# A shifted-window attention and expert block on one core: the channel norm once per token, with the normalised x, v and the gates passed through memory

## The reference

```python
x = x + _L0_conv_ref(_ln_c(x), qkv_w, lepe_w, bias_table)
t = _to_tokens(x)
t = t + _L0_ffn_ref(_ln_t(t), router_w, router_b, expert_w, expert_b)
```

## Time and profile before

| | us |
|---|---|
| median of three runs | 3803.37 |
| lowest, highest | 3798.1, 3808.32 |
| profiled execution, its own time | 3802.88 |
| its span, first to last instruction | 3801.0 |
| busy: PE, DVE, POOL, ACT | 3274.6, 3207.6, 2920.3, 2223.4 |

### The profile page before, as it was taken

The page is one execution under the profiler, slowest core; times in us unless marked ns, Lnnn a source line. Parts: engine busy times, 40 slices in busy tenths (PEclk is TensorE's granted clock), DMA queues, the critical chain, the costliest instruction groups (busy, mean ns, idle before and its releaser), DMA issues.

```text
span 3801.0 us, 207759 instructions
## 1 busy us (share of the span) xinstructions
PE 3274.6 (86%) x83621; PEld 1990.9 (52%) x83621; DVE 3207.6 (84%) x7044; ACT 2223.4 (58%) x4516; POOL 2920.3 (77%) x5385
## 2 busy tenths in 40 slices
PE   3889898888888888888888988888888898889985
PEld 1655555555555555555555555555555555555541
DVE  2789988888888888988888888888888888999983
ACT  2666655665656656565566665666565665666641
POOL 3988878787878777878787877787787878888860
PEclk8999999999999999999999999999999999999985
DMA  1232323232323222323222232322232323233221
GB/s 32 59 81 73 82 70 82 70 82 68 83 70 80 71 76 76 78 75 78 72 74 78 74 78 72 80 75 78 69 81 69 82 71 82 73 84 79 76 65 39
DMA packets 307856, 279.35 MB, mean 73 GB/s; under 512 B 122368, under 2 KB 288304, under 8 KB 306864
## 3 DMA queue, kind: packets, MB, share of 16 engines
q1 hardware_dynamic: 140976, 152.09, 15.2%
q0 software_dynamic: 165888, 113.57, 12.0%
HBM read 95.33 MB, written 56.62 MB: 40 GB/s over the span
## 4 chain that ended last, share of the span: by engine, by line
PE 25%; SPq 22%; DVE 20%; issue 16%; DMA 10%; ACT 5%; DVEq 1%; POOL 1%; POOLq 0%; ACTq 0%
SPq L401 14%; SPq L433 7%; PE bank L629 6%; DMA z2t<-z 6%; DVE lepe L929 4%; DMA z<-fin 4%; PE bank L584 3%; PE bank L634 3%; PE bank L561 3%; DVE fin L989 3%; PE bank L656 3%; DVE gx L917 2%; PE bank L543 2%; DVE prob L949 2%; ACT row_inv L701 2%
## 5 line engine op out<-in xcount | busy, mean ns | idle before, releaser
L490 POOL DMA_DIRECT2D vx<-vt x3072 | 1555.3, 515 | 623.8 <-issue 487.2
L629 PEld LDWEIGHTS bank<-probT,vx 128*32 128x32 f32 x36864 | 827.9, 191 | 254.1 <-issue 250.4
L629 PE MATMUL bank<-probT,vx 128*32 128x16 f32 x36864 | 888.7, 235 | 25.2 <-issue 23.6
L479 POOL DMA_DIRECT2D kx<-k_sb x1536 | 737.8, 488 | 119.3 <-ACT k_sb L748 100.3
L561 PEld LDWEIGHTS bank<-kx,qx 32*32 32x32 f32 x36864 | 571.6, 109 | 330.6 <-issue 326.9
L561 PE MATMUL bank<-kx,qx 32*32 32x64 f32 x36864 | 673.8, 221 | 54.3 <-issue 46.1
L929 DVE SCALAR_TENSOR_TENSOR lepe<-vpad,lepe_sb,lepe 128x384 f32<-128x384 f32 x960 | 675.8, 704 | 0.0
L917 DVE TENSOR_TENSOR gx<-bank,yn_pair 128x384 f32<-128x384 f32 x768 | 424.2, 552 | 280.6 <-PE bank L532 277.6
L543 PE MATMUL bank<-gx,expert_sb 128*64 128x384 f32 x1536 | 343.1, 526 | 173.2 <-DVE gx L917 171.3
L725 ACT ACTIVATE prob<-prob 128x512 f32<-128x512 f32 x576 | 359.8, 625 | 199.3 <-DVE prob L949 189.9
L509 POOL TENSOR_TENSOR lepe_p<-lepe_p,tap_sb 128x384 f32<-128x384 f32 x384 | 424.7, 1106 | 27.5 <-issue 6.1
(11 more groups left out here) (101 smaller groups left out, 4803.6 us busy)
## 6 DMA issues: line engine op xcount, KB each, us to landing
vx<-vt POOLq DMA_DIRECT2D x3072, 12.0 KB, 1.9
kx<-k_sb POOLq DMA_DIRECT2D x1536, 24.0 KB
yn_pair<-yn POOLq DMA_DIRECT2D x384, 96.0 KB
z<-fin SPq DMA_DIRECT2D x1344, 24.0 KB
xs<-in_x SPq DMA_DIRECT2D x96, 192.0 KB
xt<-in_x SPq DMA_DIRECT2D x192, 96.0 KB
z0t<-z SPq DMA_DIRECT2D x192, 96.0 KB
out_y<-y_out SPq DMA_DIRECT2D x192, 96.0 KB, 2.2
```

Of the source, the lines that this page charges most:

```text
L479: pool.dma_start(kx[to + m:to + C:4, r % 2, m, :], k_sb[at + m:at + C:4, r % 2, :])\
L490: pool.dma_start(vx[to:to + TOK, r % 2, g * 8 + x:g * 8 + 8:2, odd, :], vt[at:at + TOK, r % 2, x::2, :, :].rearrange("p h n k -> p h (n k)"))\
L629: last = MM(bank_o[32 * c:32 * c + 32, at * TOK:(at + 1) * TOK], vx[:, kr % 2, :, at % 2, at // 2 * 4 + c], probT[:, kr % 2, at, c * TOK:( ...
```

## The change

**The channel norm** is now done once per tile on unrolled tokens. SP loads x into a new buffer xa (two DMAs), centre, variance and the multiply run on xa once a tile in place of once a strip, SP stores the result to memory as xn (two DMAs, store_xn) and loads the strips, rolled and unrolled, from xn into xs (five DMAs, load_strips, seven slots later).

**v** goes from vt through memory: two DMAs store it into v_rows (store_v), in pieces of 192 B, and eight DMAs, in place of sixteen, load vx from there in pieces of 1536 B. vx has another order of its axes.

**The gates** are no longer split into bf16 parts. PE transposes them in fp32 (L572's place), ACT copies them, SP stores them (one DMA of 24 KB, store_gates) and loads each row into 64 partitions with four DMAs of 393 KB each (spread_gates) into gate_wide. The eight selection matmuls are gone. gx is made by four DVE operations of 768 columns on inputs that are both in SBUF, and the experts' matmuls follow by pairs. The bias is one fp32 matmul.

**load_tile** moves from SP's queue to POOL's, behind spread_k, store_v, spread_v and pair_yn and before pool_taps in a slot's list. The two additions for y are in two slots; y has four buffers. The logits are transposed into bank_g. The lags grow: the strips' steps from value on by nine slots, store_z from 15 to 24, load_tile from 24 to 34, the first use of the loaded tile from 27 to 37, tile_out from 39 to 56. DVE does gate steps 0 to 11 in the first of two slots and 12 to 16 in the second.

In the diff "..." stands where lines are left out; POOL's load_tile issues the same seven loads as SP's did.

```diff
 LAG = dict(
-    centre=0, variance=1, value=2, query_key=3,
-    spread_k=4, turn_v=5, place_bias=6, spread_v=8, score=7, shift=8,
-    turn_p=10, product=11, divide=14,
-    tap_products=6, pool_taps=7, taps=10, add_taps=15,
-    store_z=15, load_tile=24, tile_sum=27, tile_variance=28, router=29, logits=30, gates=31,
-    pair_yn=31, gap_exp=33, turn_gates=34, experts=35, tile_out=39)
+    centre=0, variance=1, store_xn=2, load_strips=9, value=11, query_key=12,
+    spread_k=13, turn_v=14, store_v=15, place_bias=15, spread_v=17, score=16, shift=17,
+    turn_p=19, product=20, divide=23,
+    tap_products=15, pool_taps=16, taps=19, add_taps=24,
+    store_z=24, load_tile=34, y_first=37, y_second=38, tile_sum=39, tile_variance=40, router=41, logits=42,
+    take_logits=43, gates=45, gap_exp=46, turn_gates=47, pair_yn=47, store_gates=48, spread_gates=50,
+    expert_bias=52, products=53, experts=54, tile_out=56)
...
+PRODUCT_AT = {(0, 1): 0, (1, 0): 1, (1, 1): 2, (2, 0): 3}
+EXPERT_AT = {(0, 0): 0, (1, 0): 1, (1, 1): 2, (2, 0): 3}
...
+        xn = nc.dram_tensor("xn", [B, C, H, W], FP32, kind="Internal").ap()
+        v_rows = nc.dram_tensor("v_rows", [2, 2, 128, 8, WIN // 2 * 4], FP32, kind="Internal").ap()
+        gate_rows = nc.dram_tensor("gate_rows", [2, GE, SPX], FP32, kind="Internal").ap()
...
-        vx = sb("vx", [128, 2, 32, 2, WIN // 2 * 4])
+        vx = sb("vx", [128, 2, 2, 32, WIN // 2 * 4])
...
-        y = sb("y", [128, 2, SPX])
+        y = sb("y", [128, 4, SPX])
...
+        gate_wide = sb("gate_wide", [128, PAIRS, 2, SPX])
...
-        gx = sb("gx", [128, 4, SPX])
+        gx = sb("gx", [128, 2, 2, SPX])
...
+            def load_x(r, im):
+                for half in range(2):
+                    at = (r % IMT * (2 * SP) + half * SP) * W
+                    sp.dma_start(xa[half * C:(half + 1) * C, r % 2, :],
+                                 x_flat[bass.ds(im, 1)][:, :, at:at + SPX].rearrange("b c n -> c (b n)"))\
+                        .then_inc(x_loaded[r % 2], 16)
...
+                if ti := s.tile("store_xn"):
+                    k, r = ti
+                    wait_alone(sp, xn_made, k + 1)
...
+                        sp.dma_start(xn_flat[im][:, :, at:at + SPX].rearrange("b c n -> c (b n)"),
+                                     xa[half * C:(half + 1) * C, r % 2, :]).then_inc(xn_stored[r % 2], 16)
+                if ti := s.tile("load_strips"):
+
+                    k, r = ti
+                    if r % IMT == 0:
+                        wait_alone(sp, xn_stored[r % 2], (k // 2 + 1) * 32)
+                    if r % IMT < IMT - 1:
+                        wait_alone(sp, xn_stored[(r + 1) % 2], ((k + 1) // 2 + 1) * 32)
+                    if s.later(r, 2):
                         wait_alone(sp, k_made, (k - 1) * 2)
-                    load_pair(r, s.image(r, IMT))
+                    im, ring, t = bass.ds(s.image(r, IMT), 1), r % 2, r % IMT
...
+                        sp.dma_start(xs[rows, 2 * ring:2 * ring + 2, :].rearrange("p a n -> p (a n)")[:, at * W:(at + n) * W],
+                                     xn_flat[im][:, src_c, row * W:(row + n) * W]
+                                     .rearrange("b c n -> c (b n)")).then_inc(xs_loaded[ring], 16)
...
+                if ti := s.tile("store_gates"):
+                    k, r = ti
+                    wait_alone(sp, gateT_saved, k + 1)
+                    if s.later(r, 2):
+
+                        wait_alone(sp, gate_spread[r % 2], k // 2 * (GATE_DMAS * 16))
+                    sp.dma_start(gate_rows[r % 2], gateT[:, r % 2, :]).then_inc(gate_stored[r % 2], 16)
+                if ti := s.tile("spread_gates"):
+                    k, r = ti
+                    wait_alone(sp, gate_stored[r % 2], (k // 2 + 1) * 16)
+                    if s.later(r, 1):
+                        wait_alone(sp, gx_made, k * PAIRS)
+                    by_expert = gate_rows[r % 2].rearrange("(f p e) n -> e f p n", f=2, e=2)
+                    for odd in range(2):
+                        for half in range(2):
+                            sp.dma_start(gate_wide[odd * C:(odd + 1) * C, :, half, :],
+                                         by_expert[odd, half].unsqueeze(0).broadcast_to([C, PAIRS, SPX]))\
+                                .then_inc(gate_spread[r % 2], 16)
...
+                if st := s.strip("store_v"):
+                    k, r = st
+                    wait_alone(pool, vt_made, k + 1)
+                    if s.later(r, 2):
+                        wait_alone(pool, v_spread[r % 2], k // 2 * (V_DMAS * 16))
+
+                    for x in range(2):
+                        pool.dma_start(v_rows[r % 2, x, :, x::2, :],
+                                       vt[:, r % 2, x::2, :, :].rearrange("p h n k -> p h (n k)"))\
+                            .then_inc(v_stored[r % 2], 16)
...
-                    wait_alone(pool, vt_made, k + 1)
+                    wait_alone(pool, v_stored[r % 2], (k // 2 + 1) * 32)
...
                     for g in range(4):
                         for x in range(2):
-                            for odd in range(2):
-                                to, at = g * CH + x * TOK, g * CH + odd * TOK
-                                pool.dma_start(vx[to:to + TOK, r % 2, g * 8 + x:g * 8 + 8:2, odd, :],
-                                               vt[at:at + TOK, r % 2, x::2, :, :].rearrange("p h n k -> p h (n k)"))\
-                                    .then_inc(v_spread[r % 2], 16)
+                            rows = v_rows[r % 2, x].rearrange("(g o k) q n -> g k o (q n)", g=4, o=2)[g]
+                            to = g * CH + x * TOK
+                            pool.dma_start(vx[to:to + TOK, r % 2, :, g * 8:(g + 1) * 8, :].rearrange("p o q n -> p o (q n)"),
+                                           rows).then_inc(v_spread[r % 2], 16)
...
+                if ti := s.tile("load_tile"):
+                    k, r = ti
...
+                    for p in range(2):
+                        wait_alone(pool, z_stored[p], counts[p] * (Z_DMAS * 16))
+                    if s.later(r, 2):
+
+                        wait_alone(pool, y_made, k - 1)
...
+                        pool.dma_start(dst[rows, r % 2, at * W:(at + n) * W],
+                                     src[im][:, :, row * W:(row + n) * W]
+                                     .rearrange("b c n -> c (b n)")).then_inc(tile_loaded[r % 2], 16)
...
-                        pe.wait_ge(gx_made, k * E + e)
-                    MM(bank_g[:, 0:SPX], expert_sel[:, e, :], gateT[:, r % 2, :], start=True, stop=True)\
-                        .then_inc(gate_spread, 1)
...
-                    pe.wait_ge(gx_made, k * E + (e + 1))
-                    if e % 2:
-                        for half in range(2):
-                            last = MM(bank_f[half * C:(half + 1) * C, 0:SPX], expert_sb[:, e // 2, :],
-                                      gx[:, (e - 1 + half) % 4, :], start=False, stop=(e == E - 1),
-                                      skip_group_check=True)
-                        last.then_inc(expert_made, 1)
-                    if e + 1 < E:
-                        spread_gate(k, r, e + 1)
+                    pe.wait_ge(gx_made, k * PAIRS + (p + 1))
+                    for half in range(2):
+                        last = MM(bank_f[half * C:(half + 1) * C, 0:SPX], expert_sb[:, p, :], gx[:, p % 2, half, :],
+                                  start=False, stop=(p == PAIRS - 1), skip_group_check=True)
+                    last.then_inc(expert_made, 1)
...
                     for blk in range(TBLK):
-                        last = MM(bank_p[0][0:3 * GE, blk * 128:(blk + 1) * 128],
-                                  gate_part[:, blk, :, :].rearrange("p a b -> p (a b)"), ident_bf[:, :],
-                                  start=True, stop=True)
+                        last = nc.tensor.transpose(bank_g[0:GE, blk * 128:(blk + 1) * 128],
+                                                   gate_tmp[:, 4, blk * GE:(blk + 1) * GE], const("ident"))
...
-                if st := s.strip("variance"):
-                    k, r = st
+                if ti := s.tile("variance"):
+                    k, r = ti
                     pe.wait_ge(sq_made, k + 1)
...
                     MM(bank_p[1][:, 0:SPX], const("mean"), sq[:, r % 2, :], start=True, stop=True).then_inc(var_made, 1)
...
+                    pe.wait_ge(xs_loaded[r // 2 % 2], (k // 4 + 1) * (XS_DMAS * 16))
...
-                if st := s.strip("centre"):
-                    k, r = st
...
-                    MM(bank_p[0][:, 0:SPX], const("centre"), xs[:, r % 4, :], start=True, stop=True).then_inc(xc_made, 1)
+                if ti := s.tile("centre"):
+                    k, r = ti
...
+                    MM(bank_p[0][:, 0:SPX], const("centre"), xa[:, r % 2, :], start=True, stop=True).then_inc(xc_made, 1)
```

(28 more changed lines are left out.)

267 lines of the change are left out of this document (117 added, 150 removed).

## The result

The changed kernel takes 4024.14 us in the median of 4 runs (4020.29 to 4031.06), beside 3800.73 us in the median of 4 runs of the kernel before: a ratio of 1.058 (95% interval 1.0555 to 1.0604), 5.8% slower, where 5% faster was forecast. The profiled execution took 4020.29 us, its span 4018.6.

The account below looks back on a forecast made before the run. Half of the tile was taken as paced by memory, half by DVE and PE. New loop: 95.5 tiles x 35.2 us + 248 us fill and drain = 3610, plus 1.9 outside the span: 3612 us, 5% faster; range 3320 to 3780.

Parts of the forecast that it names:

- The SP part: SP's queue: nine added transfers at 0.6 us, 18.0 us from even fin, so the odd strip's z stores start 2 us late.
- rival (b): Gate broadcast clogs SP's DMA rings, PE waits for xs loads if it takes over 17 us; 4060 us, chance 0.12.
- I cost the v, k, xn paths at nothing: Waits for v, xn and xs transfers to land: two or three slots cover them, so no time added.
- collision term: DVE's gx, now reading two SBUF inputs, collides with POOL's adds: 0.5 us a tile taken, at most 1.9.
- The loop: Odd fin, z stores landed 11.1, POOL 13.7, DVE 10.1: 34.9 us; with a second loop of 34.6, 35.2 a tile.
- then DVE, 10.1: Last part of the loop: DVE from its first tap to the next odd fin, 10.1 us.
- The sign of it: Sign of a right forecast: DVE waits before L929's first tap for POOL's adds, 2 to 3 us a tile.
- floor of 32.4: DVE's least time per tile: 33.1 - 2.2 + 0.5 + 1.0 (other idle time) = 32.4 us.
- Outside the steady part: Fill and drain: 193 us now plus 55 for 17 more light slots, 248 us.
- (a): DVE is the bound and POOL's chain hides: only the floor of 32.4 us remains, 3344 us; chance 0.28.
- (c): v stores cost POOL 4.1 us each, so POOL needs 42 us a tile: 4261 us; chance 0.03.
- (d): Work moves but the loop stays at 37 us through SP's waits and POOL's add: 3793 us, no change; chance 0.04.

## Why the prediction was wrong

**The failed step: the gate copies priced at their issue.** The SP part gave the four copies 0.6 us each and said "their size hardly matters to the issue". That was true (0.62 to 0.65 us) and beside the point: what they do to the other work once issued stood at nothing in the sum, and only rival (b) asked for it. 1.57 MB a tile in one burst keeps all engines full (share 0.81 and more from 1554 to 1569 us in the tile shown). Added alone to the kernel before, this traffic costs 444 us; taking three fourths of it from the kernel after gives 365 us (4024 - 3660). The forecast missed by 412 us.

**The rival that had it.** Rival (b), the broadcast clogs the rings, gave 4060 us at a chance of 0.12; it was 4024. That it came so near is luck, for its mechanism was not the one: it had PE wait for the strip loads, and PE waited 32.3 us for them in all. By its own rule PE should not have waited: the engines were full for some 15 us, under its 17. What it missed is that a full set of DMA engines delays work that has no queue in common with the copies. That PE's instructions are among it is inferred, not shown: no view gives the time at which an instruction arrives. For it speak four things. The stall falls in the middle of a group with nothing named that it waits for. It comes with full engines and not with mere lateness. DVE's five pauses, one a turn of the loop, grow from 10.1 to 39.3 us under the same traffic. And the page shows the instructions as a DMA queue of their own, q8, 10.93 MB in 667 packets, 16 KB each. The Trainium skill, Runtime: NRT & Kernel Launch, section "Instruction fetch mechanics", says that each sequencer refills itself in 16 KiB blocks by DMA and that the cost is mostly hidden. The packet size here agrees. If the inference holds, "mostly hidden" fits the kernel before (71.8 us at a share of 0.29) and not the kernel after (471.5 us at 0.58).

**PE and its clock.** The forecast had PE at 29 to 30 us a tile and 2900 us in all; it was 2690.87 / 85.4 = 31.5 us and 3094.8 us. The sum had no term for the clock, which was 0.83 and not 0.96. With two-byte gates six slots later, at 0.91, PE takes 2919.6 us.

**"I cost the v, k, xn paths at nothing."** In doubt for xn inside this change (187 us with the strip order restored, which moves more than xn) and right for it alone (no loss). Wrong for v: alone it costs some 33 us (0.8%), not by a wait for its landing. POOL's adds moved beside two-input DVE work, 211 us of DVE time, and issue grew by 76.7 us; the two were not separated. The sum had a collision term, but for a change of place only gx's.

**The loop was right in kind.** Odd fin, z stores, landing, POOL, first tap, DVE: the chain shows it. Its sizes: 40.15 for 34.9 us. The step "then DVE, 10.1" overlooked that SP waits for DVE's multiply (xa) right after the tap, and issues thirteen transfers between it and the odd z stores: 12.4 us, of which one strip load took 2.18 us to issue while the engines were full. The sign of it was there but weak: DVE waited 119.7 us for the adds, 1.3 us a tile where 2 to 3 were forecast. With the bytes halved and the loop opened by six slots the tile takes 34.8 us, with DVE 92.6% busy; the forecast had 35.2 by the loop and a floor of 32.4.

**Sizes.** gx 1048 ns in the mean (945 forecast), v stores 876 ns (0.8), vx from memory 590 (515 taken), a tap add 1211 (1106 before), fin 806 (709). POOL's busy time of 2398.75 us in 3400, or 85.4 tiles, is 28.1 us a tile for 28.8 forecast; DVE's 32.2 for 31.4 (the floor of 32.4 less its 1.0 of idle time). Each of these terms is near, and none was the matter. Outside the steady part 213.6 us for 248.

**Rivals (a), (c), (d).** (c) fell with the 876 ns. (a) and (d) did not come; DVE comes near its floor only where bytes are taken away and the second part stands six slots later (34.8 and 34.3 us a tile).

## What to carry to other kernels

A transfer has two prices, its issue and the time for which it fills the DMA engines; sum the bytes of a period and look at the share in the stretch where they come, not at the mean (0.29 became 0.45 in the mean and cost 11.6%, with 15 of 80 stretches of 2 us full; sent as two pairs it was 0.51 and 4.5%, so the mean says little). A broadcast multiplies bytes: put the saved matmuls (2.7 us of PE a tile here) against them, and halve them by type first where the result can bear the rounding. Then test each part alone: here one gained, one lost little, and the traffic of the third outweighed both.

## What the hardware showed that I had not expected

- A burst of 1.57 MB that nobody waits for costs 4.7 us a tile of 37.8; the same bytes as two pairs 1.9 us (444 and 177 us over 95.5 tiles).
- PE stands for 2.19 to 4.40 us in the middle of a group of 64 matmuls while all DMA engines are full, and its nameless idle time over the run goes from 71.8 to 471.5 us; after it the clock is 0.50, and a score takes 1.41 instead of 1.10 us.
- In its five pauses, one for each jump of the loop, DVE's nameless idle time goes from 10.1 to 39.3 us under the traffic that nobody waits for.
- Two broadcast copies over 128 partitions, first source dimension 2, run at a DMA share of 0.12 to 0.13 where nothing else runs, two of 16 engines, and are so slow that the kernel takes 6109.52 us; four over 64 partitions take 3980.73.
- yn's multiply of 518 ns takes 1658 ns when POOL's adds fall beside it, and 960 taps 840 instead of 704 ns.
